# Router logits formed inside both attentions, and a new order of the steps in linear attention

## The reference, cut to what matters

```python
x = x + conv(_gn(x))                    # adaptive and atrous depthwise convolutions, fused
x = x + box3x3(_gn(x))
t = tokens(x)                           # 16 images x 256 tokens x 128 channels
t = t + softmax_attention(_ln_t(t), Wq, bq, Wk, bk, Wv, bv, Wo, bo)     # 8 heads of 16
t = t + moe_1(_ln_t(t), router_w, w_gate, w_up, w_down)                 # 8 experts, top 2, hidden 256
t = t + linear_attention(_ln_t(t), Wq, Wkv)                             # elu + 1 features, 8 heads
t = t + moe_2(_ln_t(t), Wg, W, V, W2)                                   # 8 experts, top 2, hidden 512
```

## Time and profile before

| what | us |
|---|---|
| median of 3 runs (879.12 to 885.61) | 883.47 |
| the profiled execution: its time | 884.63 |
| the profiled execution: its span, first to last instruction | 882.9 |
| PE busy / DVE / ACT / POOL | 717.3 / 521.0 / 416.2 / 401.1 |
| first routing (from its first instruction to the first of the experts) | 302.73 to 364.98 |
| linear attention | 491.35 to 596.10 |
| second routing | 596.43 to 651.85 |

### The profile page before, as it was taken

One profiled execution on the slowest core, in us unless ns is written; L12 is line 12 of the kernel. 1 busy time (PEld: TensorE's weight loads), 2 busy tenths in 40 slices (PEclk: granted clock), 3 DMA queues, 4 the chain that ended last, 5 costly groups with the idle time before them and its releaser, 6 DMA issues. The chain is left out here.

```text
span 882.9 us, 17711 instructions
## 1 busy us (share of the span) xinstructions
PE 717.3 (81%) x5093; PEld 560.7 (64%) x5093; DVE 521.0 (59%) x1467; ACT 416.2 (47%) x1075; POOL 401.1 (45%) x436
## 2 busy tenths in 40 slices
PE   3996879899998762988999156568389999999996
PEld 1555656666665462757888145557268888888882
DVE  7447857777776358665555258885863333333334
ACT  2423436767675331565555255544244444444434
POOL 0003245556663033345664577700036676766740
PEclk9997969999998765699999688886569999999999
DMA  3001000000000051164333122205001111111118
GB/s 102 1 1 25 1 1 1 1 0 0 0 1 1 18 186 36 44 186 118 91 89 78 53 55 52 53 4 191 1 21 40 44 47 46 46 49 42 49 29 285
DMA packets 33974, 46.18 MB, mean 52 GB/s; under 512 B 8195, under 2 KB 22663, under 8 KB 33648
## 3 DMA queue, kind: packets, MB, share of 16 engines
q1 hardware_dynamic: 25040, 27.57, 9.8%
q0 software_dynamic: 8864, 17.72, 7.7%
HBM read 30.11 MB, written 15.60 MB: 52 GB/s over the span
## 5 line engine op out<-in xcount | busy, mean ns | idle before, releaser
L1986 DVE TENSOR_TENSOR f_h<-ps,f_silu 128x512 f32<-128x512 f32 x71 | 49.1, 692 | 121.5 <-ACT f_silu L1944 121.5
L1044 DVE TENSOR_REDUCE negmax<-ps 128x2 f32<-128x512 f32 x128 | 82.6, 687 | 44.3 <-PE ps L878 43.4
L1832 POOL DMA_INDIRECT f_xg<-f_normed,f_gather x71 | 68.9, 971 | 78.1 <-POOLq L1469 54.8
L1832 POOL DMA_INDIRECT d_xg<-d_normed,d_gather x71 | 67.6, 952 | 71.0 <-PE ps L1873 42.3
L1944 ACT ACTIVATE f_silu<-ps 128x512 f32<-128x512 f32 x71 | 42.4, 598 | 108.8 <-PE ps L1883 108.8
L1838 POOL DMA_INDIRECT f_results<-f_y,f_scatter x71 | 71.9, 1012 | 45.7 <-issue 32.0
L785 ACT ACTIVATE prob<-ps 128x512 f32<-128x512 f32 x128 | 69.6, 598 | 42.2 <-PE ps L897 42.1
L1262 POOL DMA_INDIRECT e_yg<-d_results,d_slot_u x64 | 61.5, 961 | 32.4 <-issue 18.6
L1904 PE MATMUL ps<-f_w_out,f_hT 128*128 x568 | 75.2, 276 | 0.6 <-DVE f_y L1992 0.6
L1904 PEld LDWEIGHTS ps<-f_w_out,f_hT 128*128 128x128 f32 x568 | 69.0, 192 | 0.9 <-issue 0.8
L1986 DVE TENSOR_TENSOR d_h<-ps,d_silu 128x256 f32<-128x256 f32 x71 | 30.0, 423 | 37.5 <-ACT d_silu L1944 36.7
(11 more groups left out here) (357 smaller groups left out, 1956.2 us busy)
## 6 DMA issues: line engine op xcount, KB each, us to landing
d_results<-d_y SPq DMA_DIRECT2D x71, 64.0 KB, 1.8
f_raw<-in_f_in SPq DMA_DIRECT2D x16, 256.0 KB, 3.0
f_ys<-f_results SPq DMA_DIRECT2D x8, 512.0 KB, 6.7
X<-in_x SPq DMA_DIRECT2D x4, 512.0 KB, 5.4
d_normed<-X SPq DMA_DIRECT2D x8, 256.0 KB, 2.0
d_raw<-in_d_in SPq DMA_DIRECT2D x8, 256.0 KB, 2.7
f_normed<-X SPq DMA_DIRECT2D x8, 256.0 KB, 2.0
f_w_out<-in_f_out SPq DMA_DIRECT2D x1, 2048.0 KB, 8.7
```

The lines of the kernel that those rows point to most:

```text
L1044: nc.vector.tensor_reduce(negmax[:, :, h // HG, col:col + 1], ps[:, 2 + h % 2, :].rearrange("p (t k) -> p t k", t=2), AX_X, ALU.max, negat ...
L1832: nc.gpsimd.indirect_dma_start(xg[:, n % 4, :], None, moe.xn_dram, bass.IndirectOffsetOnAxis(ap=moe.gather[:, n:n + 1], axis=0)).then_inc( ...
L1986: nc.vector.tensor_tensor(h[:, n % 2, :], UP(n), silu[:, n % 2, :], ALU.mult).then_inc(h_ready, 1)
```

## The change

- In `adaptive_conv` both routers are loaded, made free of their column means by a product with a matrix of 1/128 (PE, then DVE), and the first one is multiplied by Wo and by bo. Centred routers make the mean of a token drop out of its logits.
- In `softmax_attention` wv and wo become 8 columns wider: V's product also gives the logits of the layer's input, which ACT multiplies by the deviation and keeps, and the output product gives the attention's share. DVE adds both in `add_output`. The bias's share is added in the first routing (`constant`).
- In `linear_attention` PE transposes the finished tokens of each image (lag 3), ACT copies them, PE multiplies by the router (lag 4), ACT copies the logits. PE's list is written out without a loop. On DVE the division comes ahead of the gathered rows, and the heads are added in the same step (lag 2 for lag 3).
- In `route` the normalisation, transposes, products and copies ahead of the top two fall away. Mean and variance are computed by POOL, the inverse deviation by DVE between the two maxima, and the rows are normalised by ACT (even groups of 4 tiles) and POOL (odd groups) beside the top two. The gap of the two best logits is multiplied by the inverse deviation. SP loads the weights ahead of storing the rows.

The diff, cut to its core:

```diff
+def pipeline(eng, stages, items, width=4, unrolled=False):
...
+    rounds = 0 if unrolled else (end - start) // width
...
+                if pair == 1:
+                    pe.wait_ge(centred, 1)
+                if pair == 3:
+                    pe.wait_ge(folded, 1)
...
+            def centre_routers():
+                pe.wait_ge(router_in, 4 * 16)
+                pe.wait_ge(average_ready, 1)
+                nc.tensor.matmul(CENTRE, average[:], raw_routers[:].rearrange("p l e -> p (l e)"),
+                                 start=True, stop=True).then_inc(centre_ps, 1)
+
+            def fold_routers():
+                pe.wait_ge(centred, 1)
+                pe.wait_ge(bo_ready, 1)
+                pe.wait_ge(out_read, 2)
+                nc.tensor.matmul(FOLD[:, 0:Moe.E], wo_T[:], top.routers[:, 0, :], start=True, stop=True)
+                nc.tensor.matmul(FOLD[:, Moe.E:], bo_wide[:], top.routers[:, 0, :], start=True,
+                                 stop=True).then_inc(fold_ps, 1)
...
+                if pair == 2:
+                    dve.wait_ge(centre_ps, 1)
+                    nc.vector.tensor_tensor(top.routers[:].rearrange("p l e -> p (l e)"),
+                                            raw_routers[:].rearrange("p l e -> p (l e)"), CENTRE,
+                                            ALU.subtract).then_inc(centred, 1)
+                if pair == 4:
+                    dve.wait_ge(fold_ps, 1)
+                    nc.vector.tensor_copy(top.wo_router[:], FOLD[:, 0:Moe.E])
+                    nc.vector.tensor_copy(top.bo_router[:], FOLD[:, Moe.E:]).then_inc(folded, 1)
...
+            nc.gpsimd.tensor_copy(wv[:, C:], top.routers[:, 0, :])
+            nc.gpsimd.tensor_copy(wo[:, C:], top.wo_router[:]).then_inc(routers_in, 1)
...
+                                     V[:, :, 0:C].rearrange("p t (h d) -> p t h d", d=HD), ACT.Copy)
+                for t in range(2):
+                    tile = bass.ds(2 * m + t, 1)
+                    last = nc.scalar.activation(top.logits_in[:, tile, :].rearrange("p t e -> p (t e)"), V[:, t, C:],
+                                                ACT.Copy, scale=top.ln_std[:, tile])
+                last.then_inc(v_ready, 1)
...
+                    last = nc.tensor.matmul(V[:, t, :], xT[:, b, t * P:(t + 1) * P], wv[:],
...
+                tiles = bass.ds(2 * n, 2)
+                nc.vector.tensor_tensor(T[:, tiles, :], OUT[:, :, 0:C], T[:, tiles, :], ALU.add)
+                nc.vector.tensor_tensor(top.logits[:, tiles, :], OUT[:, :, C:], top.logits_in[:, tiles, :],
+                                        ALU.add).then_inc(tok_ready, 1)
...
+            def tokens_transposed(at, first, last):
+                act.wait_ge(tT_ps, at.n + 1)
+                act.wait_ge(logit_ps, at.n + 1)
+                nc.scalar.activation(tT[:, at.b, :], TT(at.b), ACT.Copy).then_inc(tT_ready, 1)
+
+            def logits(at, first, last):
+                act.wait_ge(logit_ps, at.n + 3)
+                nc.scalar.activation(top.logits[:, bass.ds(2 * at.n, 2), :].rearrange("p t e -> p (t e)"),
+                                     LOGITS(at.b), ACT.Copy).then_inc(logit_ready, 1)
+
+            pipeline(act, [(-1, transposed), (0, parts), (3, tokens_transposed), (-2, normed), (-3, rstds),
+                           (4, logits)], N, 2)
...
+                pe.wait_ge(tT_ready, at.n + 1)
...
-            pipeline(pe, [(-1, transpose), (0, project), (2, output), (1, sum_tokens)], N, 2)
+            pe.sem_inc(tT_ready, 2)
+            pe.sem_inc(logit_ready, 2)
+
+            def transpose_tokens(at, first, last):
+                pe.wait_ge(tok_ready, at.n + 3)
+                pe.wait_ge(logit_ready, at.n + 1)
+                for t in range(2):
+                    ins = nc.tensor.transpose(TT(at.b)[:, t * P:(t + 1) * P],
+                                              T[:, bass.ds(2 * at.n + t, 1), :].rearrange("p t c -> p (t c)"), ident[:])
+                ins.then_inc(tT_ps, 1)
+
+            def token_logits(at, first, last):
+                pe.wait_ge(tT_ready, at.n + 3)
+                for t in range(2):
+                    ins = nc.tensor.matmul(LOGITS(at.b)[:, t * Moe.E:(t + 1) * Moe.E], tT[:, at.b, t * P:(t + 1) * P],
+                                           top.routers[:, 1, :], start=True, stop=True)
+                ins.then_inc(logit_ps, 1)
+
+            pipeline(pe, [(3, transpose_tokens), (-1, transpose), (0, project), (2, output), (4, token_logits),
+                          (1, sum_tokens)], N, 2, True)
...
-            pipeline(dve, [(-2, shifts), (0, features), (1, sums), (-3, combine_first), (-3, moments),
-                           (2, normalise), (3, add_tokens), (3, statistics)], N, 4)
-
-
-def route(nc, top, moe, router_dram, w_out_dram, split=None):
+            pipeline(dve, [(-2, shifts), (0, features), (1, sums), (2, normalise), (-3, combine_first), (-3, moments),
+                           (2, add_tokens), (2, statistics)], N, 4)
...
-            sp.dma_start(router[:], router_dram).then_inc(router_in, 16)
-
-            groups = moe.xn_dram.rearrange("(p g t) c -> g p t c", p=P, t=GROUP)
-            for g in range(TILES // GROUP):
-                sp.wait_ge(xn_ready, g + 1)
-                sp.dma_start(groups[g], xn[:, g * GROUP:(g + 1) * GROUP, :]).then_inc(xn_stored, 16)
             sp.dma_start(moe.w_out[:], w_out_dram).then_inc(moe.weights_in, 16)
             if split is not None:
                 for i in range(split.pieces):
                     split.load(sp, i)
+            groups = moe.xn_dram.rearrange("(p g t) c -> g p t c", p=P, t=GROUP)
+            for g in range(TILES // GROUP):
+                sp.wait_ge((xn_even, xn_odd)[g % 2], g // 2 + 1)
+                sp.dma_start(groups[g], xn[:, g * GROUP:(g + 1) * GROUP, :]).then_inc(xn_stored, 16)
...
+            stats = top.ln_stats
+            difference, spread = moment[:, 0, :], moment[:, 1, :]
+            nc.gpsimd.tensor_tensor(spread, stats[:, :, 2], stats[:, :, 5], ALU.add)
+            nc.gpsimd.tensor_tensor(top.ln_mean[:], stats[:, :, 1], stats[:, :, 4], ALU.add)
+            step(nc.gpsimd.tensor_tensor(difference, stats[:, :, 1], stats[:, :, 4], ALU.subtract))
+            nc.gpsimd.tensor_scalar(spread, spread, 1.0 / C, None, ALU.mult)
+            nc.gpsimd.tensor_scalar(difference, difference, 0.5, None, ALU.mult)
+            step(nc.gpsimd.tensor_scalar(top.ln_mean[:], top.ln_mean[:], 0.5, None, ALU.mult))
+            step(nc.gpsimd.tensor_tensor(difference, difference, difference, ALU.mult))
+            nc.gpsimd.tensor_tensor(top.ln_std[:], spread, difference, ALU.add).then_inc(var_ready, 1)
...
+            pool.wait_ge(rstd_ready, 1)
+            for g in range(1, TILES // GROUP, 2):
+                for t in range(g * GROUP, (g + 1) * GROUP):
+                    ins = nc.gpsimd.tensor_scalar(xn[:, t, :], T[:, t, :], top.ln_mean[:, t:t + 1],
+                                                  top.ln_rstd[:, t:t + 1], ALU.subtract, ALU.mult)
+                ins.then_inc(xn_odd, 1)
...
+            act.wait_ge(var_ready, 1)
+            nc.scalar.activation(top.ln_std[:], top.ln_std[:], ACT.Sqrt, bias=top.eps5[:]).then_inc(std_ready, 1)
+            act.wait_ge(shift_ready, 1)
+            for g in range(0, TILES // GROUP, 2):
+                for t in range(g * GROUP, (g + 1) * GROUP):
+                    ins = nc.scalar.activation(xn[:, t, :], T[:, t, :], ACT.Identity, bias=ln_shift[:, t:t + 1],
+                                               scale=top.ln_rstd[:, t:t + 1])
+                ins.then_inc(xn_even, 1)
...
-            norm_on_vector(dve)
-            with dve.Fori(0, 2) as i:
-                for t in range(TILES // 2):
-                    tile = i * (TILES // 2) + t
-                    ins = nc.vector.tensor_scalar(
-                        xn[:, bass.ds(tile, 1), :].rearrange("p t c -> p (t c)"),
-                        T[:, bass.ds(tile, 1), :].rearrange("p t c -> p (t c)"),
-                        top.ln_mean[:, bass.ds(tile, 1)], top.ln_rstd[:, bass.ds(tile, 1)], ALU.subtract, ALU.mult)
-                    if t % GROUP == GROUP - 1:
-                        ins.then_inc(xn_ready, 1)
             dve.wait_ge(consts_ready, 1)
-            dve.wait_ge(logit_ready, TILES // GROUP + 2)
             by_tile = lambda ap: ap.unsqueeze(2).broadcast_to([P, TILES, E])
             by_expert = lambda ap: ap.unsqueeze(1).broadcast_to([P, TILES, E])
+            if constant is not None:
+                step(nc.vector.tensor_tensor(logits[:], logits[:], by_expert(constant[:]), ALU.add))
...
+                    dve.wait_ge(std_ready, 1)
+                    nc.vector.reciprocal(top.ln_rstd[:], top.ln_std[:]).then_inc(rstd_ready, 1)
+                    dve.wait_ge(rstd_ready, 1)
+                    nc.vector.scalar_tensor_tensor(ln_shift[:], top.ln_mean[:], -1.0, top.ln_rstd[:], ALU.mult,
```

(53 more changed lines are left out.)

89 lines of the change are left out of this document (28 added, 61 removed).

## The result

The changed kernel takes 925.56 us in the median (924.48 to 926.19) beside 884.38 for the kernel before on the same chip (879.12 to 885.61): ratio 1.048, 95% interval 1.043 to 1.052. The profiled execution has a span of 922.8 us against 882.9. The sign was right, the size not: 903 had been forecast, with 916 as the upper end.

| stage | before | after | forecast difference | measured |
|---|---|---|---|---|
| to the first routing | 302.8 | 302.8 | +1.7 | 0.0 |
| first routing, to the experts' first gather | 63.0 | 52.1 | -12.5 | -10.9 |
| experts, to linear attention's first gather | 126.2 | 126.8 | 0 | +0.6 |
| linear attention | 104.4 | 167.6 | +43.1 | +63.1 |
| second routing, to the experts' first gather | 56.0 | 41.7 | -12.7 | -14.3 |

A forecast was written before the change was run, and what follows sets the result against it. POOL and DVE were taken to bound linear attention together, with PE busy 81% of the span. Terms: 884.6 + 0.7 (conv) + 1.0 (softmax) - 25.2 (routing) + 43.1 (linear attention) = 904.2, less 1.16: 903 us; range 888 to 916.

The forecast's parts named there:

- the ring's turn: Linear attention: addition, PE, ACT, DVE, addition close once per image, taking 8.4 us where a step took 5.22; stage +43.1.
- PE starts at A + 0.07: Linear attention: PE begins the token transposes 0.07 us after A, the end of DVE's addition.
- PE waits for ACT rather than for the addition: Linear attention: a sign that would show the forecast wrong; PE's longest wait was expected to be for DVE's addition.
- the 4.34 us of the earlier trace: Linear attention before: PE from transpose to end of token sum, taken as low clock, against 2.66 otherwise.
- The upper end of the range, 9.06 a turn: Linear attention: turn with PE at low clock throughout, stage +53, 913 us; a rival with chance 0.15.
- 3.4 + 2.3 + 1.75: Linear attention's end: step without projection; last division and addition; then last transpose, copy, logits and copy, in us.
- Counted wherever it stands: Linear attention: moving DVE's division (0.88 us) ahead saves nothing, since it lies in the ring anyway.
- Lead-in 3.3 us: Both routings: time until DVE's first top-two step, waiting for POOL's constants behind eight new operations; before, 20.16 and 19.90.
- The tile: Both routings: POOL normalises one tile in 0.35 us, between a quarter of 0.77 and all of it; 16 per routing.
- The 0.51 us lost per us of POOL: Routing: DVE's loss beside POOL's work, read from the weight splits; charged to the tiles as 2.9 us per routing.
- list building slower by some 3 us: Both routings: a sign expected if the forecast holds, beside a first top-two step some 3.3 us after the start.
- The rival of late stores: Routing: stores come late or POOL's tiles hold DVE much more; routing gain 18.5, 910 us; chance 0.07 (the rest).

The follow-up runs named there:

- experiment 2: The changed kernel with ACT's copy of the logits ahead of the inverse deviation in linear attention: 917.1 us, ratio 1.036 to the kernel before.
- Experiment 1: The changed kernel with PE's projections and head products ahead of the token transposes in linear attention: 887.5 us, ratio 1.005 to the kernel before.
- experiments 1 and 6: The second: Experiment 1's kernel with DVE's division back behind the gathered rows and moments: 874.9 us, ratio 0.993 to the kernel before.
- experiment 8: The changed kernel with all 32 normalised tiles of both routings on ACT, none on POOL: 916.8 us, ratio 1.041 to the kernel before.

## Why the prediction was wrong in size

- **The step that failed is the ring's turn.** Forecast 8.4 us between 7.57 and 9.06, measured 10.3. Three parts of the 1.9 us: (a) "PE starts at A + 0.07" overlooked that the token transposes also wait for a logits' copy, which ACT does only behind the inverse deviation: A + 0.86, 0.79 us, shown by experiment 2. The prediction had named "PE waits for ACT rather than for the addition" as what would prove it wrong. (b) It took a turn partly at low clock; the burst was low nearly in full, 9.06 - 8.4 = 0.66. (c) At low clock the burst from transposes to mask is 5.99 us where 5.48 had been worked out, 0.5 too little. Most of that is a misread row: the 4.34 us of the earlier trace rows were taken for low clock, but that burst had a granted clock of 0.61, and its Q took 0.73 us. In the ring the same part of the burst takes 4.71, at 0.50 from 568.46 to 573.07. The added transposes and logits take 0.46 and 0.72 (from start to start) for 0.4 and 0.7. The upper end of the range, 9.06 a turn, was no bound, since (a) and (c) were missing in it. (With 9.06 the prediction's own terms give 43.1 + 13 x 0.66 = 51.7 for the stage, not the 53 that it states.)
- **Where the 20 us lie.** The ten turns with gathered rows took 100.8 us from addition to addition for 84, since the first of them were shorter than 10.3: 16.8 us. The three behind them took 19.7 for 19.2. The end of the stage, behind the addition of the third last image, took 11.1 for 3.4 + 2.3 + 1.75 = 7.45: 3.7 us that the ring's turn doesn't explain, each of its three terms being too small (5.15, 3.13, 2.8 measured). What stretched them wasn't separated.
- **The ring itself was right.** Experiment 1 takes the projections out of it and gets 38 us back. The three late turns without gathered rows had been worked out implicitly as 7.57 - 2.01 = 5.56 at full clock; two of them took 11.47 us at granted clock 1.00, 5.74 each.
- **The division.** "Counted wherever it stands" is right in the ring through the addition. That a second ring through the moments exists, in which its place does matter, wasn't seen; in the changed kernel the larger ring covers it, and it cost some 8 us alone, and 12.6 by the medians or 10 by the ratios once the projections were out of the first ring (experiments 1 and 6).
- **Routing.** Lead-in 3.3 us forecast, 3.5 measured in both. Eight operations of POOL took 0.24 to 0.31 us each (0.25 forecast). The tile was put at 0.35 us and takes 0.795 (12.72 for 16), a little more than the 0.77 row that had been the upper bound. The 0.51 us lost per us of POOL, read from the splits, doesn't hold for the tiles: 1.6 us are lost beside 12.72 (second routing, experiment 8). So there the two errors partly cancelled, 1.6 for the 2.9 us forecast. In the first routing the splits, pushed back by the tiles, left the top-two stage, where they had cost 7.3 us, and met the list building; "list building slower by some 3 us" was right in kind and is 8.8 there (six pairs of splits at 1.47 us each) and nothing in the second routing. The rival of late stores didn't come about: the first gather starts 1.1 us after VectorE's last list entry in the first routing and 1.7 in the second, in both kernels.
- **Conv and softmax.** +1.7 forecast, 0.0 in one profile each; the start of the first routing differs by several microseconds among the profiles of these kernels (296 to 305), so a term of this size is neither shown nor refuted.

The Trainium skill (SBUF — State Buffer, section Who interferes with whom) has VectorE's instructions with two SBUF inputs and GpSimd's that read SBUF exclude each other for the whole instruction. One row agrees in full: a sum on 128x6 took 1.23 us beside POOL's 1.26, where the one on 128x7 before it took 0.16. The rows of the list stage nearly agree: the engines end in turn, DVE at 331.31, POOL at 331.78, DVE at 332.85, POOL at 334.00, DVE at 334.60. From one end to the next there passes the instruction's time alone (0.61, 1.22, 1.26 and 0.75 us) less 0.11 to 0.15, so a group is 3.29 us and not the sum of 3.84. The tiles don't agree: VectorE lost 1.6 us beside 12.72, where the prediction's sum by this rule had charged every microsecond.

## What to carry to other kernels

Before an instruction that waits is put at the head of an engine's list, follow the whole list behind it until it comes back to what is waited for: the length of that ring is the least that a step can take, however little the added work. List every semaphore that the moved instruction waits for, the buffer releases too, and ask on the releasing engine what stands ahead of the release. And work that is taken off one engine's queue moves what stands behind it in the other's: look at what the delayed part will meet.

## What the runs showed of the hardware that I had not expected

In this ring the higher clock was granted in the pauses (0.82 to 0.83) and the lower one in the bursts (0.55 to 0.56), so that a mean clock of 0.66 over nine steps hides that nearly all products ran at 1.2 GHz. Filling the pauses with four products a step raised it to 0.87, yet seven of eleven turns still stood at 0.80 to 0.83.

POOL's normalised tile costs as much as a product with four times its elements. The line's view in the changed kernel (ns: least, median, most):

```profile
L1664 POOL TENSOR_SCALAR X<-T,ln_mean,ln_rstd x32: 787/797/952, 309.9 to 667.9; 128x128 f32<-128x128 f32 x32
```

The 128x512 operation with two per-partition scalars takes 770 ns, there into another number type. A price by the number of elements was therefore the wrong way to reach from one to the other; what the tile's time goes by instead wasn't tried.
